# Active-expert loop with the next block's transposes, split and first products issued in the current block, and first weights loaded in routing

## The chip, the cores and the metric

The kernel runs on one core of one Trainium2 chip. The metric is device time in microseconds (us) of one execution; the figure for a kernel is the median of its runs.

## The reference, cut to what matters

Sixteen sequences of 512 tokens of width 256 (8192 tokens) pass an adaptive layer norm and attention, then a second one and a mixture of experts. Only the latter is touched by the change:

```python
logits = x @ Wr + br                                  # 8 experts
top_vals, top_idx = jax.lax.top_k(logits, TOPK)       # TOPK = 2
w = jax.nn.softmax(top_vals, axis=-1)
cap = max(int(math.ceil(N / E * CF)), 1)              # 1280
kv, ki = jax.lax.top_k(key_mat, cap)                  # per expert, its cap largest weights
tok = flat_tok[ki]
gate = jnp.where(valid, w_flat[ki], 0.0)
h1 = jax.nn.gelu(einsum('ech,ehf->ecf', x[tok], W1) + b1, approximate=False)
y = einsum('ecf,efh->ech', h1, W2) + b2
out = jnp.zeros_like(x).at[tok.reshape(-1)].add((y * gate[..., None]).reshape(-1, H))
```

W1 is 256 x 1024 and W2 1024 x 256 for each expert, in float32. The router's weights are small (0.001) beside its bias, so with the inputs drawn here the two experts with the largest bias, numbers 2 and 4, take the tokens. Each is full at its capacity of 1280. The others get none.

## The kernel before

The program is written engine by engine; semaphores set the order between engines, and each engine runs its own instructions in the order written. Stages follow one another behind a barrier: `setup`, `attention`, `route`, `experts`, `last_norm`.

`route` finds each expert's tokens. On VectorE (DVE) it computes keys, then the 1280th largest key of each expert in 15 steps of counting, then the number of blocks per expert (L1059 to L1063), then the table INFO (L1066 to L1076): for each of the eight experts the number of its blocks, the blocks before it, and the active experts before it. A loop of one-hot products on TensorE, with operands from DVE and GpSimd (POOL), then gives the list IDX of token numbers (L1093 to L1106).

`experts` works in blocks of 256 tokens (BLK), five for a full expert. `each` (L1154) is the loop that every engine runs: over all eight experts, three reads from INFO each, and for those with blocks an optional `expert` part, then an inner loop of `block` parts. A counter g numbers the blocks across experts. A `Stream` (L37) is a semaphore that is waited for with a value computed from g.

Each matrix is kept as the sum of a high part (float32r) and a low part. `hi_lo_matmul` (L89) makes three matmuls of one product. An expert's part: SyncE (SP) loads W1F and W2F (1 MB each), ScalarE (ACT) writes the high parts W1H and W2H, DVE the low parts W1L and W2L. A block's part:

- POOL (L1210) copies the token numbers to TOKG, gathers the tokens' rows to XG (two indirect DMAs) and their keys to GK (two more). Then it waits for YS of the block before and adds it to `acc_rows` in HBM with two accumulating scatters by the token numbers TOKS. Each scatter is waited for before the next one is issued. `gate(j)` (L1194) is a tiny POOL operation that carries waits.
- TensorE (L1302) transposes XG to PSUM (four), then `mm1(f)` for eight columns of W1 and, two steps behind, `mm2(f)` with W2. Both are groups of six matmuls.
- DVE (L1267) splits the transposed tokens into XTH and XTL, takes the gates from GK, makes YB = b2 x gate, splits each gelu output HF into HH and HL, and finally writes YS = y x gate + YB (L1295).
- ACT (L1249) applies gelu, with a load of the activation tables before a block's first one.

On TensorE the order within a block is this:

```python
for f in range(FC + 2):
    if f < FC:
        mm1(f)
    if f >= 2:
        mm2(f - 2)
```

Its first `mm1` waits for XTL, so for transposes and split, and its transposes stand behind the last `mm2` of the block before.

Of the kernel before, what the change touches and what calls it, by code (L numbers as in the profile page):

```python
# [17 lines left out]
F32, F32R = mybir.dt.float32, mybir.dt.float32r  # L18
# [92 lines left out]
def build_program(nc, ap, out):  # L111
    top = ExitStack()
    with top:
# [33 lines left out]
        m["INFO"] = sb("INFO", [1, 4 * E], I32)  # L147
# [683 lines left out]

def route(nc, ap, m, sem, sb):
# [34 lines left out]
    NBR, NBD = sb("NBR", [1, 6, E]), sb("NBD", [P, E])  # L867
    ktab = m["ktab_dram"]
# [3 lines left out]
    s_db, s_ab, s_oe = sem("s_rdb"), sem("s_rab"), sem("s_roe")  # L872
# [9 lines left out]
    with nc.Block() as block:  # L882
# [41 lines left out]
        @block.sync  # L924
        def _(sp):
            sp.wait_ge(s_key, TC)
# [42 lines left out]
        def _(dve):  # L969
# [97 lines left out]
            nb, act_, cum, cua, z = (NBR[:, j, :] for j in range(5))  # L1067
            link(dve.tensor_copy(nb, nb_ps[0:1, :]))
            link(dve.tensor_scalar(act_, nb, 0.0, None, ALU.is_gt))
            link(dve.memset(z, 0.0))  # L1070
            link(dve.tensor_tensor_scan(cum, nb, z, 0.0, ALU.add, ALU.add))
            link(dve.tensor_tensor_scan(cua, act_, z, 0.0, ALU.add, ALU.add))
            link(dve.tensor_tensor(cum, cum, nb, ALU.subtract))
            link(dve.tensor_tensor(cua, cua, act_, ALU.subtract))
            for j, row in enumerate((nb, cum, cua)):
                link(dve.tensor_copy(m["INFO"][:, j * E:(j + 1) * E], row))  # L1076
# [34 lines left out]
def experts(nc, ap, m, sem, sb):  # L1111
# [4 lines left out]
    GATES_USED = 4 + BT  # L1116
    assert CAP % BLK == 0

    W1F, W2F = sb("W1F", [P, KC, F]), sb("W2F", [P, FC, D])
# [3 lines left out]
    B1R, B1, B2 = sb("B1R", [E * FC, P]), sb("B1", [P, E * FC]), sb("B2", [P, E, D])  # L1123

    XG, GK, TOKG, TOKS = sb("XG", [P, BT, D]), sb("GK", [P, BT, E]), sb("TOKG", [P, BT], U32), sb("TOKS", [P, BT], U32)
# [10 lines left out]
    s_w1, s_w2 = S("fw1", 1, 16), S("fw2", 1, 16)  # L1136
# [3 lines left out]
    s_tokg, s_toks = S("ftokg", BT), S("ftoks", 1)  # L1140

    s_t, s_m1, s_m2, s_gate, s_yb = S("ft", 1), S("fm1", FC), S("fm2", FC), S("fgate", BT), S("fyb", BT)
    s_xh, s_xl, s_gelu, s_hh, s_hl, s_y = S("fxh", KC), S("fxl", KC), S("fgelu", FC), S("fhh", FC), S("fhl", FC), S("fy", BT)
    s_init, s_b, s_b1t, s_b1 = sem("finit"), sem("fb"), sem("fb1t"), sem("fb1")
# [9 lines left out]
    def each(eng, expert, block):  # L1154


        with eng.Fori(0, E) as e:
            nb = eng.value_load(INFO[0:1, bass.ds(e, 1)], min_val=0, max_val=MAXB)
            g0 = eng.value_load(INFO[0:1, bass.ds(e + E, 1)], min_val=0, max_val=E * MAXB)
            a = eng.value_load(INFO[0:1, bass.ds(e + 2 * E, 1)], min_val=0, max_val=E)  # L1160
            with eng.If(nb > 0):
                if expert is not None:
                    expert(e, a, g0)
                if block is not None:
                    with eng.Fori(0, nb) as k:
                        block(e, a, g0 + k, k)

    with nc.Block() as blk:
        @blk.sync
        def _(sp):  # L1170
            w1 = ap["L0_ffn_W1"].rearrange("e (k p) f -> p (e k) f", p=P)
            w2 = ap["L0_ffn_W2"].rearrange("e (f p) n -> p (e f) n", p=P)
            sp.dma_start(B1R[:, :], ap["L0_ffn_b1"].rearrange("e (f p) -> (e f) p", p=P)).then_inc(s_b, 16)
            sp.dma_start(B2[:, :, :], ap["L0_ffn_b2"].partition_broadcast(P)).then_inc(s_b, 16)

            def expert(e, a, g):
                k_row, f_row = sp.snap(e * KC), sp.snap(e * FC)

                s_w1l.wait(sp, a, -1)
                s_w1.done(sp.dma_start(W1F[:, :, :], w1[:, bass.ds(k_row, KC), :]))  # L1180
                s_w2l.wait(sp, a, -1)
                s_w2.done(sp.dma_start(W2F[:, :, :], w2[:, bass.ds(f_row, FC), :]))
            each(sp, expert, None)

        @blk.gpsimd
        def _(pool):
            start(pool, streams)

            pool.iota(TOKS[:, :].bitcast(I32), pattern=[[0, BT]], base=NT, channel_multiplier=1).then_inc(s_init, 1)
            pool.memset(YS[:, :, :], 0.0).then_inc(s_init, 1)  # L1190
            pool.memset(GATE[:, :], 0.0).then_inc(s_init, 1)
            pool.wait_ge(s_init, 3)
# [5 lines left out]
            def scatter(g):  # L1198


                s_y.wait(pool, g, -1)
                for t in range(BT):
                    if t:
                        s_sc.wait(pool, g, t - 1)
                    gate(4 + t)
                    off = bass.IndirectOffsetOnAxis(ap=TOKS[:, t:t + 1], axis=0)
                    s_sc.done(pool.indirect_dma_start(out=m["acc_dram"], out_offset=off, in_=YS[:, t, :], in_offset=None,
                                                      compute_op=ALU.add))

            def block(e, a, g, k):  # L1210

                s_toks.wait(pool, g, -1)
                gate(0)
                for t in range(BT):
                    s_tokg.done(pool.tensor_copy(TOKG[:, t:t + 1], IDX[:, bass.ds(e * (CAP // P) + k * BT + t, 1)]))
                s_tokg.wait(pool, g, BT - 1)
# [10 lines left out]

                scatter(g)
# [237 lines left out]
```

## Time and profile before

| | us |
|---|---|
| median of 3 runs | 1643.86 |
| lowest and highest | 1641.98, 1646.58 |
| profiled execution: its own time | 1649.5 |
| its span | 1647.7 |
| TensorE matmuls busy | 1333.9 (81%) |
| DVE busy | 1141.7 (69%) |
| ACT busy | 742.3 (45%) |
| POOL busy | 531.9 (32%) |

Times in the profile count from the start of the span. The page cuts the span into 40 slices and gives each engine's busy tenths. The timeline lists instructions in order of time with the idle time before each and what ended it; "issue" is idle time in which the engine waited for nothing that the profile shows. A POOL row DMA_INDIRECT is the time in which POOL writes the descriptors, not the transfer. TensorE's granted clock (PEclk) is 1.00 or 0.50 of full speed, or a mean of the two over a window.

### The profile page before, as it was taken

The page shows a single profiled execution, that of the slowest core. Times are in us where ns is not written, and L with a number is a line of the kernel's source. Part 1 is how long each engine was busy: PE and PEld are TensorE (multiplying, and loading weights), DVE is VectorE, ACT ScalarE, POOL GpSimd, SP SyncE. Part 2 cuts the span into 40 slices and gives each one's busy share as a digit, 9 for nine tenths or more (in the row PEclk, how much of TensorE's full clock was granted, in tenths as well). Part 3 has the DMA queues.
Part 4 walks back from the last instruction along what each step waited for, and adds up shares of the span by engine and source line. Part 5 has one row for each costly group of instructions (what it writes and reads, how often), then busy time and mean ns, then how long its engine had stood idle before and what let it go on. Part 6 is the DMA issues. An engine that isn't in the chain of part 4 may idle for free. (4 is left out here: it accounts for less than half of the span.)

```text
span 1647.7 us, 24318 instructions
## 1 busy us (share of the span) xinstructions
PE 1333.9 (81%) x5919; PEld 946.5 (57%) x5920; DVE 1141.7 (69%) x2504; ACT 742.3 (45%) x1433; POOL 531.9 (32%) x853
## 2 busy tenths in 40 slices
PE   5499999999999999999999999998311948868200
PEld 3366666666666666666666666665211947867200
DVE  2478778777787778787787877875377525555387
ACT  2365656556566565565655657544000013232052
POOL 1111413324234232342323413313300544455147
PEclk8699999999999999999999999999555558988655
DMA  4000011010010110101101011011000032111364
GB/s 107 14 13 27 3 51 52 0 51 26 26 51 0 52 41 11 52 0 51 52 0 51 0 39 40 1 39 39 26 6 1 0 104 62 27 32 29 111 215 143
DMA packets 66758, 67.90 MB, mean 41 GB/s; under 512 B 13504, under 2 KB 62832, under 8 KB 66560
## 3 DMA queue, kind: packets, MB, share of 16 engines
q1 hardware_dynamic: 42960, 42.72, 8.6%
q10 hardware_dynamic: 18960, 18.88, 3.4%
q0 software_dynamic: 4768, 5.59, 2.2%
q14 instruction: 53, 0.43, 0.1%
q8 instruction: 17, 0.28, 0.1%
HBM read 38.25 MB, written 28.66 MB: 41 GB/s over the span
## 5 line engine op out<-in xcount | busy, mean ns | idle before, releaser
L827 PE MATMUL PS<-PF,V 128*128 128x512 f32 x1024 | 524.0, 594 | 0.0
L558 ACT ACTIVATE PF<-PS 128x512 f32<-128x512 f32 x512 | 302.9, 595 | 345.4 <-PE PS L753 343.7
L730 DVE TENSOR_REDUCE NMAX<-PS 128x1 f32<-128x512 f32 x512 | 346.4, 686 | 160.1 <-PE PS L762 149.7
L752 PE MATMUL PS<-Q,K 128*128 128x512 f32 x512 | 405.8, 793 | 0.9 <-ACT PF L558 0.9
L528 POOL TENSOR_TENSOR XL<-XF,XH 128x512 fp32r<-128x512 f32 x64 | 84.2, 1315 | 445.6 <-ACT XH L633 445.6
L762 PE MATMUL PS<-K,Q 128*128 128x512 f32 x512 | 203.3, 398 | 6.9 <-DVE NMAX L730 6.2
L753 PE MATMUL PS<-Q,K 128*128 128x512 f32 x512 | 202.7, 396 | 0.0
L827 PEld LDWEIGHTS PS<-PF,V 128*128 128x128 f32 x1024 | 174.5, 189 | 36.2 <-issue 6.6
L576 ACT ACTIVATE Q<-PS 64x512 fp32r<-64x512 f32 x256 | 151.5, 592 | 64.8 <-PE PS L93 60.0
L752 PEld LDWEIGHTS PS<-Q,K 128*128 128x128 f32 x512 | 97.2, 190 | 123.5 <-issue 105.6
L753 PEld LDWEIGHTS PS<-Q,K 128*128 128x128 f32 x512 | 97.4, 190 | 121.7 <-issue 121.6
L762 PEld LDWEIGHTS PS<-K,Q 128*128 128x128 f32 x512 | 96.6, 189 | 31.6 <-DVE NMAX L730 8.6
L669 DVE STREAM_TRANSPOSE RECT<-PS 64x512 f32<-64x512 f32 x128 | 91.9, 718 | 13.0 <-PE PS L827 9.2
L520 POOL TENSOR_TENSOR NLO<-TR,NHI 128x512 fp32r<-128x512 f32 x32 | 41.1, 1286 | 163.9 <-DVE NHI L714 163.9
L698 DVE TENSOR_TENSOR Q<-PS,Q 64x512 fp32r<-64x512 f32 x128 | 87.7, 685 | 7.7 <-ACT Q L576 4.7
L681 DVE TENSOR_TENSOR XF<-PS,RECT 64x512 f32<-64x512 f32 x128 | 87.2, 681 | 7.6 <-DVE RECT L675 4.6
L675 DVE STREAM_TRANSPOSE RECT<-RDEN 64x512 f32<-64x512 f32 x128 | 89.1, 696 | 1.0
L536 POOL TENSOR_TENSOR H<-H,MODB 128x256 f32<-128x256 f32 x64 | 47.0, 734 | 109.1 <-ACT H L625 109.1
L91 PE MATMUL PS<-GH,XH 128*128 128x256 f32 x256 | 74.0, 289 | 6.4 <-POOL XL L528 4.6
L93 PE MATMUL PS<-GH,XL 128*128 128x256 f32 x256 | 73.5, 287 | 0.0
L92 PE MATMUL PS<-GL,XH 128*128 128x256 f32 x256 | 73.5, 287 | 0.0
L91 PE MATMUL PS<-XTH,W1H 128*128 128x256 f32 x160 | 51.6, 323 | 24.6 <-DVE XTL L1274 23.3
(272 smaller groups left out, 2463.1 us busy)
## 6 DMA issues: line engine op xcount, KB each, us to landing
X<-in_L_attn_x SPq DMA_DIRECT2D x16, 512.0 KB, 5.0
MODB<-mod_rows SPq DMA_DIRECT2D x16, 512.0 KB, 4.5
h_rows<-H ACTq DMA_DIRECT2D x16, 512.0 KB, 3.4
acc_rows<-H ACTq DMA_DIRECT2D x16, 512.0 KB, 4.1
A<-acc_rows SPq DMA_DIRECT2D x16, 512.0 KB, 9.1
out_x<-X SPq DMA_DIRECT2D x16, 512.0 KB, 2.9
Q<-MROW SPq DMA_DIRECT2D x128, 2.0 KB
W1F<-in_L_ffn_W SPq DMA_DIRECT2D x2, 1024.0 KB
```

The lines of the kernel that those rows point to most:

```text
L91: eng.matmul(out, lhs[0], rhs[0], start=first, stop=False)
L558: s_exp.done(act.activation(PF[:, u % 4, :], st_bank(u), ACT.Exp))
L576: s_qhi.done(act.activation(Q1[half * R:(half + 1) * R, 2 * idx + odd, :], bank[odd * R:(odd + 1) * R, :], ACT.Copy))
L669: s_x.done(dve.transpose(RECT[:, :], bank[R:P, :]))
L675: s_x.done(dve.transpose(RECT[:, :], RDEN[:, :].unsqueeze(2).broadcast_to([R, T // 32, 32])))
L681: s_x.done(dve.tensor_tensor(XF[odd * R:(odd + 1) * R, p % 2, :], bank[0:R, :], RECT[:, :], ALU.mult))
L698: s_qlo.done(dve.tensor_tensor(Q2[0:R, h, :], bank[odd * R:(odd + 1) * R, :], Q1[odd * R:(odd + 1) * R, h, :].bitcast(F32), ALU.subtract))
L730: s_mred.done(dve.tensor_reduce(NMAX[:, h % 2, c:c + 1], mx_bank(u), AX.X, ALU.max, negate=True))
L752: pe.matmul(st_bank(u), K1[:, kp, keys], Q1[:, h, :], start=True, stop=False)
L753: s_st.done(pe.matmul(st_bank(u), K2[:, kp, keys], Q2[:, h, :], start=False, stop=True))
L762: s_mx.done(pe.matmul(mx_bank(u), Q1[:, h, c * P:(c + 1) * P], K1[:, kp, :], start=True, stop=True))
L827: s_pv.done(pe.matmul(pv_bank(h), V1[:, vp, c, :], PF[:, u % 4, :], start=(c == 0), stop=(c == TC - 1)))
```

## The change

- The table INFO now lists the active experts only, in order: number, blocks less one, and blocks before; then the count of active experts and of blocks. An active expert has at least two blocks. DVE computes it with more small operations.
- In `route`, SP loads the biases (B1R, B2) at the start and the first active expert's W1F and W2F once INFO is written. Later SP loads the next expert's weights when the low parts of the current ones are made (after the last one, it loads once more, a transfer that no product uses).
- `each` loops over active experts: a `first` part, `middle` for all blocks but the last, and `last`, a second copy of the block's code.
- TensorE does the next block's transposes in the middle of the current block (behind `mm1(4)`), and its `mm1(0)` and `mm1(1)` behind the current block's last `mm2`. DVE splits the next block's tokens before YS. The gates are taken behind f = 2.
- POOL keeps the token numbers of two blocks more (TOKG to TOKP to TOKQ to TOKS). Its turn g gathers for block g and scatters block g-2, the first scatter ahead of the GK gathers. Two turns without gathers follow the last block. DVE writes YS of block g when turn g+1 has scattered block g-1.
- ACT runs a one-column activation (DUMMY) at the start of each part, so that the load of the tables stands there.

The core of the diff:

```diff
+            sp.wait_ge(s_info, 1)
+            e = sp.value_load(m["INFO"][0:1, 0:1], min_val=0, max_val=E - 1)
+            w1, w2 = weight_rows(ap)
+            k_row, f_row = sp.snap(e * KC), sp.snap(e * (F // P))
+            m["s_w1"].done(sp.dma_start(m["W1F"][:, :, :], w1[:, bass.ds(k_row, KC), :]))
+            m["s_w2"].done(sp.dma_start(m["W2F"][:, :, :], w2[:, bass.ds(f_row, F // P), :]))
...
+    def each(eng, first, middle, last):
+        with eng.Fori(0, actives(eng)) as a:
+            e = eng.value_load(INFO[0:1, bass.ds(a, 1)], min_val=0, max_val=E - 1)
+            more = eng.value_load(INFO[0:1, bass.ds(a + E, 1)], min_val=1, max_val=MAXB - 1)
+            g0 = eng.value_load(INFO[0:1, bass.ds(a + 2 * E, 1)], min_val=0, max_val=E * MAXB)
+            if first is not None:
+                first(e, a, g0)
+            with eng.Fori(0, more) as k:
+                middle(e, a, g0 + k, k)
+            last(e, a, g0 + more, more)
...
+            def shift(g):
+                s_toks.wait(pool, g, -1)
+                gate(4 + BT)
+                s_tokg.done(pool.tensor_copy(TOKQ[:, :], TOKP[:, :]))
+                s_tokg.wait(pool, g, 0)
+                gate(5 + BT)
+                s_tokg.done(pool.tensor_copy(TOKP[:, :], TOKG[:, :]))
+                s_tokg.wait(pool, g, 1)
+                gate(6 + BT)
+            def take(g):
+                s_toks.done(pool.tensor_copy(TOKS[:, :], TOKQ[:, :]))
+                s_toks.wait(pool, g, 0)
+                s_y.wait(pool, g, -BT - 1)
...
+                shift(g)
...
+                take(g)
+                scatter(g, 0)
...
+                for t in range(1, BT):
+                    s_sc.wait(pool, g, t - 1)
+                    scatter(g, t)
+                s_gx.wait(pool, g, 0)
+                s_gk.wait(pool, g, 0)
+                gate(0)
...
+                if more:
+                    split_tokens(g + 1)
...
+                s_sc.wait(dve, g + 1, BT - 1)
...
+            def expert(e, a, g):
+                transposes(g)
                 s_w1l.wait(pe, a, 0)
...
+                mm1(g, 0)
+                mm1(g, 1)
...
+            def block(e, a, g, more):
+                for f in range(2, FC):
+                    mm1(g, f)
+                    if f == 4 and more:
+                        transposes(g + 1)
+                    mm2(a, g, f - 2)
+                mm2(a, g, FC - 2)
+                mm2(a, g, FC - 1)
+                if more:
+                    mm1(g + 1, 0)
+                    mm1(g + 1, 1)
```

POOL in the block's loop, before. GATEp is the tile of `gate`, the names in brackets are the semaphores waited for (fsc: a scatter has landed, fy: YS is written, fgate: the gates are read):

```order
L1196 TENSOR_TENSOR GATEp<-GATEp 128x1 [waits ftoks]
...
L1215 COPY TOKG<-IDX 128x1
...
L1196 TENSOR_TENSOR GATEp<-GATEp 128x1 [waits ft,ftokg]
L1221 DMA XG<-h_rows,TOKG 128x256 x2
...
L1196 TENSOR_TENSOR GATEp<-GATEp 128x1 [waits fgate]
L1226 DMA GK<-key_rows,TOKG 128x8 x2
L1196 TENSOR_TENSOR GATEp<-GATEp 128x1 [waits fy]
L1207 DMA acc_rows<-YS,TOKS 8320x256
...
L1196 TENSOR_TENSOR GATEp<-GATEp 128x1 [waits fsc]
L1207 DMA acc_rows<-YS,TOKS 8320x256
...
L1196 TENSOR_TENSOR GATEp<-GATEp 128x1 [waits fsc]
L1231 COPY TOKS<-TOKG 128x2
```

and now:

```order
L1245 COPY TOKQ<-TOKP 128x2
...
L1231 TENSOR_TENSOR GATEp<-GATEp 128x1 [waits ftokg]
L1248 COPY TOKP<-TOKG 128x2
...
L1231 TENSOR_TENSOR GATEp<-GATEp 128x1 [waits ftokg]
...
L1268 DMA XG<-h_rows,TOKG 128x256 x2
L1254 COPY TOKS<-TOKQ 128x2
...
L1231 TENSOR_TENSOR GATEp<-GATEp 128x1 [waits fy]
L1238 DMA acc_rows<-YS,TOKS 8320x256
...
L1231 TENSOR_TENSOR GATEp<-GATEp 128x1 [waits fgate]
L1275 DMA GK<-key_rows,TOKG 128x8 x2
...
L1231 TENSOR_TENSOR GATEp<-GATEp 128x1 [waits fsc]
L1238 DMA acc_rows<-YS,TOKS 8320x256
```

The first scatter has moved ahead of the GK gathers, and the wait for it (fsc) behind them. Two copies and their gates are new before the XG gathers, and one copy behind them.

TensorE around a block's edge, before. The last second group, and the next turn of the loop:

```order
L91 MATMUL PS<-W2H,HH 128x256 [waits fhl]
L92 MATMUL PS<-W2L,HH 128x256
L93 MATMUL PS<-W2H,HL 128x256
...
L1165 REGISTER_ALU
L1165 COMPARE_AND_BRANCH
...
L1307 MATMUL PS<-IDENT,XG 128x128 [waits fxl]
L1307 MATMUL PS<-IDENT,XG 128x128 x3
...
L91 MATMUL PS<-XTH,W1H 128x256 [waits fxl]
L92 MATMUL PS<-XTL,W1H 128x256
```

and now:

```order
L91 MATMUL PS<-W2H,HH 128x256 [waits fhl]
L92 MATMUL PS<-W2L,HH 128x256
L93 MATMUL PS<-W2H,HL 128x256
...
L91 MATMUL PS<-XTH,W1H 128x256 [waits fxl]
L92 MATMUL PS<-XTL,W1H 128x256
L93 MATMUL PS<-XTH,W1L 128x256
...
L91 MATMUL PS<-XTH,W1H 128x256 [waits fgelu]
L92 MATMUL PS<-XTL,W1H 128x256
L93 MATMUL PS<-XTH,W1L 128x256
...
L1200 REGISTER_ALU
L1200 COMPARE_AND_BRANCH
```

The next block's first groups (they wait for fxl, the low part of its tokens) follow the last second group directly, with no transposes between, and the loop turns behind them. The transposes stand between `mm1(4)` and `mm2(2)`.

## Rows read from the trace of the kernel before

**Rows 1.** The page's 40 slices of 41.2 us: busy tenths of TensorE.

```profile
PE   5499999999999999999999999998311948868200
```

**Rows 2.** Timeline, DVE, POOL: start, duration (us), instruction, [idle before, releaser].

```profile
1335.92 0.24 DVE L1106 SCALAR_TENSOR_TENSOR IDX<-PS,LF 128x80 uint32<-128x80 f32 x1
...
1540.37 0.18 POOL L1196 TENSOR_TENSOR GATEp<-GATEp 128x1 f32<-128x1 f32 x1 [2.39 <-DMA acc_rows<-YS,TOKS]
```

**Rows 3.** Waits, 1337 to 1545 us: total us, times, longest.

```profile
POOL GATEp L1196 <- DMA acc_rows<-YS,TOKS: 49.3, 21, 2.9
...
PE PS L91 <- DVE XTL L1274: 23.3, 9, 4.7
```

**Rows 4.** Timeline, TensorE: the inner turn, and one group in mid-block.

```profile
1375.44 0.60 PE L1307 MATMUL PS<-IDENT,XG 128*128 128x128 f32 x4
...
1434.29 0.28 PE L91 MATMUL PS<-XTH,W1H 128*128 128x256 f32 x1
...
1435.00 0.28 PE L91 MATMUL PS<-W2H,HH 128*128 128x256 f32 x1
```

**Rows 5.** Timeline, DVE: YS of blocks 0 and 4 (starts of ten such rows).

```profile
1375.70 0.88 DVE L1295 SCALAR_TENSOR_TENSOR YS<-PS,GATES,YB 128x256 f32<-128x256 f32 x2 [1.14 <-PE PS L93]
...
1441.95 0.88 DVE L1295 SCALAR_TENSOR_TENSOR YS<-PS,GATES,YB 128x256 f32<-128x256 f32 x2 [1.13 <-PE PS L93]
```

**Rows 6.** Windows: us, busy by engine, PEclk, DMA share, GB/s.

```profile
1411.00:1427.00 16.00, 13.94 (x100) 13.29 (x100) 7.58 (x24) 4.96 (x9) 8.04 (x15) 0.89 0.21 33
1468.00:1486.00 18.00, 12.90 (x103) 12.01 (x101) 9.87 (x30) 4.86 (x9) 9.21 (x16) 1.00 0.19 30
```

**Rows 7.** Timeline, POOL: one turn, blocks 1 and 2.

```profile
1385.15 0.18 POOL L1196 TENSOR_TENSOR GATEp<-GATEp 128x1 f32<-128x1 f32 x1 [2.35 <-DMA acc_rows<-YS,TOKS]
...
1386.84 1.02 POOL L1221 DMA_INDIRECT XG<-h_rows,TOKG  x1 [0.33 <-issue]
...
1389.16 0.21 POOL L1196 TENSOR_TENSOR GATEp<-GATEp 128x1 f32<-128x1 f32 x1
...
1392.88 0.19 POOL L1196 TENSOR_TENSOR GATEp<-GATEp 128x1 f32<-128x1 f32 x1 [1.08 <-DVE YS L1295]
...
1397.24 0.18 POOL L1196 TENSOR_TENSOR GATEp<-GATEp 128x1 f32<-128x1 f32 x1 [2.40 <-DMA acc_rows<-YS,TOKS]
...
1401.43 0.18 POOL L1196 TENSOR_TENSOR GATEp<-GATEp 128x1 f32<-128x1 f32 x1 [2.23 <-DMA acc_rows<-YS,TOKS]
```

**Rows 8.** Timeline, DVE in routing: 64 elements; INFO table begins, ends.

```profile
1190.75 0.22 DVE L991 TENSOR_TENSOR DENr<-M 128x64 f32<-128x64 f32 x1
...
1269.06 0.15 DVE L1068 COPY NBR<-PS 1x8 f32<-1x8 f32 x1 [1.50 <-PE PS L954]
...
1270.92 0.69 DVE L1080 TENSOR_REDUCE D<-PS 128x64 f32<-128x512 f32 x1
```

**Rows 9.** Timeline, POOL and TensorE: first gate, first product.

```profile
1345.94 0.19 POOL L1196 TENSOR_TENSOR GATEp<-GATEp 128x1 f32<-128x1 f32 x1 [7.14 <-issue]
...
1360.66 0.58 PE L91 MATMUL PS<-XTH,W1H 128*128 128x256 f32 x1 [4.22 <-DVE XTL L1274]
```

**Rows 10.** Timeline, POOL and TensorE: a gather waited for.

```profile
1513.35 1.26 POOL L1221 DMA_INDIRECT XG<-h_rows,TOKG  x1 [0.47 <-issue]
...
1517.91 0.65 PE L1307 MATMUL PS<-IDENT,XG 128*128 128x128 f32 x4 [0.27 <-DMA XG<-h_rows,TOKG]
```

**Rows 11.** Timeline, TensorE: second expert's first products, half clock.

```profile
1453.00 0.58 PE L91 MATMUL PS<-XTH,W1H 128*128 128x256 f32 x1 [4.72 <-DVE XTL L1274]
...
1453.60 0.41 PE L93 MATMUL PS<-XTH,W1L 128*128 128x256 f32 x1
1453.81 0.41 PE L91 MATMUL PS<-XTH,W1H 128*128 128x256 f32 x1
```

**Rows 12.** Groups by line, 1337:1545: busy us, mean ns, idle before.

```profile
L1307 PE MATMUL PS<-IDENT,XG 128*128 128x128 f32 x40 | 7.1, 307 | 18.1 <-DMA XG<-h_rows,TOKG 12.8 <-issue 5.3
...
L1263 DVE TENSOR_TENSOR W1L<-W1F,W1H 128x2048 fp32r<-128x2048 f32 x2 | 4.6, 2292 | 22.0 <-issue 17.3 <-ACT W1H L1245 4.6
```

More of the change, by code:

```diff
@@ L1152, in y_bank, with actives @@
         return PS[:, 5 + t, 0:D]
[L1154 to L1166, printed above, removed]
+    def actives(eng):
+        return eng.value_load(INFO[0:1, 3 * E:3 * E + 1], min_val=1, max_val=E)
+    def each(eng, first, middle, last):
[8 more added lines that the diff above has]
+            last(e, a, g0 + more, more)
     with nc.Block() as blk:
@@ L1194, in gate, with scatter @@
             def gate(j):
                 pool.tensor_tensor(GATE[:, j:j + 1], GATE[:, GATES_USED:], GATE[:, GATES_USED:], ALU.add)
[L1198 to L1208, printed above, removed]
+            def scatter(g, t):
+                gate(4 + t)
+                off = bass.IndirectOffsetOnAxis(ap=TOKS[:, t:t + 1], axis=0)
+                s_sc.done(pool.indirect_dma_start(out=m["acc_dram"], out_offset=off, in_=YS[:, t, :], in_offset=None,
+                                                  compute_op=ALU.add))
@@ L1308, in block @@
                 s_t.done(last)
-                s_w1l.wait(pe, a, 0)
-                def mm1(f):
-                    s_gelu.wait(pe, g, max(f - 4, -1))
-                    cols = slice(f * P, (f + 1) * P)
-                    for c in range(KC):
-                        if f == 0:
-                            s_xl.wait(pe, g, c)
-                        last = hi_lo_matmul(pe, h_bank(f), (W1H[:, c, cols], W1L[:, c, cols]),
-                                            (XTH[:, c, :], XTL[:, c, :]), c == 0, c == KC - 1)
-                    s_m1.done(last)
@@ L1321, in mm2 @@
-                def mm2(f):
-                    if f == 0:
-                        s_w2l.wait(pe, a, 0)
-                        s_y.wait(pe, g, -1)
-                    s_hl.wait(pe, g, f)
-                    for t in range(BT):
-                        rows = slice(t * P, (t + 1) * P)
-                        last = hi_lo_matmul(pe, y_bank(t), (HH[:, f % 4, rows], HL[:, f % 4, rows]),
-                                            (W2H[:, f, :], W2L[:, f, :]), f == 0, f == FC - 1)
-                    s_m2.done(last)
@@ L1331, in block, with mm1 @@
-                for f in range(FC + 2):
-                    if f < FC:
-                        mm1(f)
-                    if f >= 2:
-                        mm2(f - 2)
+            def mm1(g, f):
+                s_gelu.wait(pe, g, f - 4)
+                cols = slice(f * P, (f + 1) * P)
+                for c in range(KC):
+                    if f == 0:
+                        s_xl.wait(pe, g, c)
+                    last = hi_lo_matmul(pe, h_bank(f), (W1H[:, c, cols], W1L[:, c, cols]),
+                                        (XTH[:, c, :], XTL[:, c, :]), c == 0, c == KC - 1)
+                s_m1.done(last)
@@ new lines, in mm2, with expert @@
+            def mm2(a, g, f):
+                if f == 0:
+                    s_w2l.wait(pe, a, 0)
+                    s_y.wait(pe, g, -1)
+                s_hl.wait(pe, g, f)
+                for t in range(BT):
+                    rows = slice(t * P, (t + 1) * P)
+                    last = hi_lo_matmul(pe, y_bank(t), (HH[:, f % 4, rows], HL[:, f % 4, rows]),
+                                        (W2H[:, f, :], W2L[:, f, :]), f == 0, f == FC - 1)
+                s_m2.done(last)
+            def expert(e, a, g):
+                transposes(g)
+                s_w1l.wait(pe, a, 0)
+                mm1(g, 0)
+                mm1(g, 1)
@@ L1338, in _ @@
             pe.wait_ge(s_b1, 1)
[L1339 removed]
+            each(pe, expert, lambda e, a, g, k: block(e, a, g, True), lambda e, a, g, k: block(e, a, g, False))
 def last_norm(nc, out, m, sem, sb):
```

152 lines of the change are left out of this document (92 added, 60 removed).

## The prediction, made before the changed kernel was run

> **What bounds the kernel now.** The page's 40 slices come first [rows 1]: TensorE is full until slice 29, idle in routing, then busy for 6 to 8 tenths over the experts. The change lies there and in a few routing rows. The experts stage runs from IDX at 1336.2 us to the landing of the last scatter (gate before it at 1540.37, plus 4.2 as below: 1544.6) [rows 2]: 208 us for ten blocks of 256 tokens, five for each of two experts. The waits of that stretch [rows 3] name two pairs: TensorE waits 23.3 us for XTL, and POOL waits 49.3 us, 21 times, for its scatters. So the next views are both timelines.
>
> TensorE: a group of six matmuls takes 0.71 us at full clock (1434.29 to 1435.00) [rows 4]. A block has 16 groups and four transposes (0.6): 12.0 us. But YS to YS is (1441.95 - 1375.70)/4 = 16.6 us [rows 5]. The 4.6 us between are the hole at the block's edge: transposes, split, first product, and gelu with its table load before the first second product. A stretch at half clock in most blocks adds to it (0.89 granted in one window, 1.00 in another) [rows 6].
>
> POOL: one turn goes from the gate at 1385.15 to that at 1401.43 [rows 7]. It is 1.7 us to the first gather, 2.3 for two XG gathers, 2.6 for two GK gathers, then 4.36 and 4.2 for the scatters, each waited for until it lands (2.4 and 2.2 us idle), with 1.08 idle for YS ahead of them. So POOL alone needs 15.2 us. It hides just behind 16.6; a faster TensorE meets it at once.
>
> **The change, part by part.**
> Routing. The INFO table takes DVE from 1269.06 to 1270.92: ten small operations, 0.18 us apart [rows 8]. Now there are eleven such (2.0), two and then three of 64 elements (0.22 for that size, 0.25 with the gap: 1.25), a reduction of 192 (between 0.22 for 64 and 0.69 for 512: 0.4) and a cast (0.2): 3.85. DVE has no idle before the next operation, so all of it is path: **+2.0**; with every new operation at 0.18 it is +1.3, with all six larger ones at 0.4 about +3. The weight and bias transfers issued there meet no other large one, and SP's wait for INFO holds only SP: nothing.
>
> Head. POOL's table walk passes the inactive experts 0 and 1, nine loads in the 7.14 us ahead of its first gate [rows 9]: 0.8 us each. Now there are four: -4.0. With +2.0 and 0.1 for the second IOTA, the first turn starts at 1344.0. W1F has landed in routing, and W1H and W1L are done before XG, which is last: first gather at 1346.4, landed 4.3 later (1513.35 to 1517.91 shows 4.56 with issues slower by 0.3 [rows 10]), transposes 1.1, split 0.8. The first product comes near 1353 where it was 1360.66 [rows 9].
>
> POOL's new turn. The GK gathers (2.6) now stand between the two scatters and fill the 2.4 us wait: -2.4. Two copies (0.26 with their wait) and net two gates (0.2) are added: +1.0, of it 0.65 before the first gather. The new waits for gx and gk fall inside the second scatter's wait: nothing; without that cover they would cost no more than one gate. So 15.2 - 2.4 + 1.0 = **13.8 us**. Bounds: 12.6 where the overlap is whole and the additions are free, 16.2 where nothing overlaps. I take 13.8: the same instructions go to the same queue, only their order differs, and their issue times are the most regular rows of the trace.
>
> TensorE's new cycle. The next block's split and first products are ahead of the block's edge. XTL comes some 0.5 late, behind HL of f = 7, so TensorE needs 12.5 us of its own. Gelu's table load (1.28) runs while the last three second groups do (2.1): hidden. But the transposes in block g need XG of g+1, and these are gathered in the POOL turn that starts when YS of g-1 may be written: 2.35 + 4.3 after that, then 0.6 and nine groups of 0.71: 13.65. YS comes 0.3 behind, which POOL does not need for another 4.7 us. So POOL's turn sets the period, 13.8 where 16.6 was, and TensorE waits about 2.5 us for XG. A half-clock stretch after it costs up to 1.7 us and is taken from the next wait.
>
> **The sum**, in the profile's time. Turn 0 is 0.6 longer, for one scatter wait of 2.9 instead of 2.3 while weights land [rows 3]: 1344.0 + 14.4 = 1358.4. Five more turns: 1427.4. YS of block 4 has waited for that and ends at 1428.4. The second expert starts cold: three loads 2.3, W1L 2.3 [rows 12], half the split 0.8, first product at 1433.8. (Before, YS at 1441.95 to the product at 1453.00 was 11.0 [rows 5, 11]; now it is 6.3, from 1427.5.) Three groups at half clock, six matmuls of 0.213 each [rows 11], take 3.8; gelu 0.65, HH and HL 0.71 and gates 0.3 follow: 1439.3. Turn 6 holds GK until these gates are read; then 2.6, 0.3 and 4.2, so it ends at 1446.5 where 1441.2 was possible. Three turns: 1487.9. The two late turns have no gathers: 0.8 for a load, 1.85, 0.35 and 8.6 give 11.6, the second 10.7. The last YS is ready for it: 1488.9 + 0.75 + 13 x 0.71 + 1.3 = 1500.2. Landing at 1510.2 instead of 1544.6: **-34.4 us**, some two thirds of it from the period. The last stage only moves.
>
> The profiled execution took 1649.5 us (its span is 1647.7), 5.6 over the median of 1643.86. On the median that makes 1643.86 - 34.4 = **1609.5 us**. Within 0.3% (5 us) a measurement of this kernel cannot tell a change from none.
>
> **The rivals.**
> (a) No overlap: the gathers behind an accumulating scatter delay it, or the wait moves to the second scatter. The turn goes up to 16.2: 9 x 2.4 = +22, 1631; with half of it 1620. For it: a wait of 2.9 beside other traffic [rows 3]. Against: the experts' transfers use 0.19 to 0.21 of the DMA engines' time [rows 6].
> (b) POOL's turn is shorter and TensorE's 12.5 or 12.7 rules: 9 x 1.1 = -10, 1599.5. For it: no row shows an added copy above 0.26. Against: the walk of waits around them has its own register work.
> (c) TensorE loses time at each loop turn. At the outer turn it sat idle 5.3 us with nothing but issue to blame [rows 12]; at the inner turn there is no gap: the transposes at 1375.44 carry no idle time [rows 4]. If the longer code brought 5.3 to each of 8 inner turns, the cycle would be 17.8: 8 x 4.0 = +32, 1641.5, no change. Against: the inner body keeps its 100 matmuls. The Trainium skill (Runtime: NRT & Kernel Launch, Instruction fetch mechanics) says that a taken branch to a page outside the fetched window stalls for a fetch. By that rule the outer body, doubled, could pay once at its turn back, and the sum would rise by one such idle time, to 1615; no row here separates a fetch from the table loads at that place.
> (d) **Slower**: the clock. Two shorter waits in a block, for YS and for XG, replace one long one, and TensorE may stay at its lower level (1.2 GHz). A block of 16 groups of 1.28 plus 1.1 is 21.6 us: 9 x 7.8 = +70, 1680. It decides once a period passes 13.8 + 34.4/9 = 17.6, with over half of each block at half clock (12.5 + 9.1 x 0.56). Against: with a hole in every block, the clock granted was still 0.89 and 1.00 [rows 6].
>
> **How the numbers follow.** The forecast, with turns of 13.3 to 14.6 (1605 to 1617), has 0.62; (a) 0.17; (b) 0.15; (c) 0.03; (d) 0.03. The range 1598 to 1625 holds the forecast, (b) and about half of (a). Faster: the forecast, (a) and (b), 0.93, rounded down for what I have not thought of; same 0.04; slower 0.03.
>
> **What would show it.** Right: the gate before the second scatter no longer idles for acc_rows, only the one behind it; almost no idle for YS on POOL; YS 13.8 us apart; TensorE waits for XG, not for XTL; the first product near 1353; YS of block 4 to the next product near 6 us; turn 6 stretched by the gates. Wrong: YS under 13 us apart (b), idle for acc_rows twice in a turn (a), issue idle at each inner turn (c), a granted clock under 0.7 over the blocks (d).

## The result, and the profile after

The changed kernel takes **1625.22 us** (median of 4 runs, 1621.00 to 1628.07) against 1645.15 us for the kernel before in the same set (4 runs, 1641.98 to 1646.58): a ratio of 0.9879, 95% interval 0.9852 to 0.9907. It is faster, and the gain is 19.9 us where 34.4 were forecast. In a later set of runs it took 1625.31 us against 1650.50 us (0.9852, 0.9835 to 0.9869): 25.2 us. The two medians of the kernel after lie within a microsecond; those of the kernel before lay between 1642.5 and 1651.0 (1642.5 and 1645.8 on chip 0, 1650.5 to 1651.0 on chips 5 and 6).

The stage itself can be read more exactly than the whole. From the write of IDX to the first load of the accumulated rows the profile before has 1551.03 - 1335.92 = 215.1 us, the one after 189.9 us, so the change is worth **25.2 us** in its stage. The table INFO ahead of that stretch costs 2.1 us more than before (the rows stand with the two kernels run again, below), which leaves 23.1 us. The forecast for the same stretch was 178.7 us (landing at 1510.2, 6.4 us to that load, IDX at 1337.9). These are the ends of it after, from the timelines of VectorE, GpSimd and SyncE (columns as in [rows 2]):

```profile
1338.27 0.24 DVE L1136 SCALAR_TENSOR_TENSOR IDX<-PS,LF 128x80 uint32<-128x80 f32 x1
...
1521.50 0.18 POOL L1231 TENSOR_TENSOR GATEp<-GATEp 128x1 f32<-128x1 f32 x1 [2.25 <-DMA acc_rows<-YS,TOKS]
1528.14 26.64 SPq L1463 DMA_DIRECT2D A<-acc_rows  x16
```

The page's line of TensorE's 40 slices, beside [rows 1]: the stage of the experts is fuller where it was 6 to 8 tenths, and one slice in its middle, the change of expert, is still low.

```profile
PE   6499999999999999999999999999511595979200
```

The waits from 1340 to 1530 us, beside [rows 3]:

```profile
POOL GATEp L1231 <- DMA acc_rows<-YS,TOKS: 29.6, 16, 2.4
...
PE PS L1382 <- DMA XG<-h_rows,TOKG: 22.6, 7, 14.4
...
PE PS L91 <- DVE XTL L1337: 11.0, 10, 8.5
DVE YS L1370 <- DMA acc_rows<-YS,TOKS: 7.9, 3, 6.4
```

GpSimd waits 29.6 us for its scatters where it waited 49.3, TensorE 11.0 us for XTL where it waited 23.3, and there is no line for GpSimd waiting for YS (8.4 us at most once, 31.1 in all before). TensorE now waits for XG: of its 22.6 us, 14.4 are the start, and 8.2 fall in six later places, where the kernel before had 0.3 in one. Of the 11.0 us for XTL, 8.5 are one wait at the change of expert. One turn of GpSimd, from its timeline, beside [rows 7]:

```profile
1375.04 0.53 POOL L1231 TENSOR_TENSOR GATEp<-GATEp 128x1 f32<-128x1 f32 x2 [2.31 <-DMA acc_rows<-YS,TOKS]
...
1377.37 1.01 POOL L1268 DMA_INDIRECT XG<-h_rows,TOKG  x1 [0.42 <-issue]
...
1379.78 0.20 POOL L1254 COPY TOKS<-TOKQ 128x2 uint32<-128x2 uint32 x1
1380.14 0.20 POOL L1231 TENSOR_TENSOR GATEp<-GATEp 128x1 f32<-128x1 f32 x1 [0.17 <-POOL TOKS L1254]
1380.86 1.62 POOL L1238 DMA_INDIRECT acc_rows<-YS,TOKS  x1 [0.52 <-issue]
...
1382.96 1.00 POOL L1275 DMA_INDIRECT GK<-key_rows,TOKG  x1 [0.16 <-issue]
...
1385.24 0.21 POOL L1231 TENSOR_TENSOR GATEp<-GATEp 128x1 f32<-128x1 f32 x1
1385.61 1.62 POOL L1238 DMA_INDIRECT acc_rows<-YS,TOKS  x1 [0.16 <-issue]
...
1389.35 0.53 POOL L1231 TENSOR_TENSOR GATEp<-GATEp 128x1 f32<-128x1 f32 x2 [1.84 <-DMA acc_rows<-YS,TOKS]
```

The gate at 1385.24, ahead of the second scatter, has no idle time for acc_rows any more: the GK gathers cover the first scatter's flight in full. But the turn is 14.31 us, not 13.8. The reader should see two idle times that the sum did not have: 0.17 before the gate at 1380.14 and 0.52 before the first scatter; in the kernel before, the gate of [rows 7] at 1392.88 was followed by its scatter after 0.15.

YS comes 13.5, 14.3, 14.3 and 17.4 us apart in the first expert. The last of these waits for the scatter of a GpSimd turn that has walked the outer loop on its way; VectorE's row and GpSimd's row at that place:

```profile
1420.57 0.44 POOL L1231 TENSOR_TENSOR GATEp<-GATEp 128x1 f32<-128x1 f32 x1 [2.28 <-issue]
...
1435.45 0.88 DVE L1370 SCALAR_TENSOR_TENSOR YS<-PS,GATES,YB 128x256 f32<-128x256 f32 x2 [6.39 <-DMA acc_rows<-YS,TOKS]
```

Laid beside the forecast, the starts of GpSimd's turns (the gate behind a landing) give the whole miss of the stage:

| part | forecast | measured | difference |
|---|---|---|---|
| first gate | 1344.0 | 1344.1 | +0.1 |
| turn 0 | 14.4 | 15.8 | +1.4 |
| turns 1 to 4 | 55.2 | 58.2 | +3.0 |
| turn 5 (outer turn in it) | 13.8 | 17.4 | +3.6 |
| turn 6 | 19.1 | 19.6 | +0.5 |
| turns 7 to 9 | 41.4 | 43.6 | +2.2 |
| two late turns | 22.3 | 22.8 | +0.5 |
| last landing | 1510.2 | 1521.5 | +11.3 |

### The profile page after: what moved, and what is told of

Read it like the earlier page. It is cut to its first block and busy times, and to the rows that moved or that the text cites. A ratio compares the mean times of both kernels' runs of the same rounds, so it can differ in the third digit from the quotient of the medians.

```text
span 1623.7 us, 24084 instructions
## 1 busy us (share of the span) xinstructions
PE 1327.1 (82%) x5919; PEld 937.7 (58%) x5920; DVE 1145.3 (71%) x2512; ACT 740.7 (46%) x1442; POOL 556.0 (34%) x928
## 5 line engine op out<-in xcount | busy, mean ns | idle before, releaser
L1318 ACT ACTIVATE HF<-PS,B 128x256 f32<-128x256 f32 x80 | 37.9, 474 | 104.0 <-PE PS L93 94.2
L922 POOL TENSOR_TENSOR OA<-OE,TOK 128x640 f32<-128x640 f32 x16 | 33.1, 2071 | 115.3 <-DVE OE L1127 115.3
```

## The experiments

The two theories that the first eight runs tell apart. **P**: GpSimd's turn still sets the period, and the missing 11 us are in its turns. **T**: TensorE (with VectorE behind it) is already the bound, and the forecast overrated what it can do. Beside each time stands, as "stage", the time from IDX to the first load of the accumulated rows in that run's profile (189.9 for the kernel after), since it does not depend on where the program's start happened to end. Two profiles of one kernel differ in it by 0.4 to 1.1 us (188.8 in the second profile of the kernel after). The runs were taken in sets on different chips, so two medians of different sets are compared with more caution than two stages.

### The GK gathers ahead of the scatters again

```diff
+                s_gate.wait(pool, g, -1)
+                gate(2)
+                for t in range(BT):
...
                 take(g)
                 scatter(g, 0)
-                s_gate.wait(pool, g, -1)
-                gate(2)
-                for t in range(BT):
...
```

> Edit: GpSimd issues the two GK gathers ahead of the first scatter again, in the kernel after; nothing else moves. Theory P (GpSimd's turn sets the period of the blocks, 14.3 us from landing to landing): about 2.4 us of issue no longer lie beside the first scatter's flight, the turn grows to 16.3 to 16.7, the gate before the second scatter idles for acc_rows again (some 1.9 to 2.1 us), and the time grows by 17 to 22 us over the kernel after, to about 1644, so nearly the whole gain of the change is gone. Theory T (TensorE or VectorE sets 14.3, and GpSimd has slack): the waits move, the time stays within 3 us of the kernel after.

Measured: 1655.50 us (5 runs), ratio 1.0079 (1.0060 to 1.0097), stage 216.7 us. This is slower than the kernel before, also in the stage (215.1 and 215.5 us there): the whole gain of the change hangs on this order. By the medians it is 13 us slower, by the stage and the table only 3 to 4; the rest lies outside both and is open, as for the medians further down. The rows of GpSimd's timeline in that kernel show the idle time of a scatter's flight back before each second scatter (2.20 before the gate at 1381.93), as in [rows 7]:

```profile
1378.11 1.62 POOL L1238 DMA_INDIRECT acc_rows<-YS,TOKS  x1 [0.51 <-issue]
1381.93 0.18 POOL L1231 TENSOR_TENSOR GATEp<-GATEp 128x1 f32<-128x1 f32 x1 [2.20 <-DMA acc_rows<-YS,TOKS]
```

Six of the nine intervals of YS are 16.5 to 17.2 us, some 2.4 more than after. The 26.8 us of the stage (30.3 by the medians) are more than the 17 to 22 expected. Turn 0 grew by 5.5 us, with waits of 2.4 and 4.6 for its two scatters, and turn 6 by 3.8, because the first GK gather now stands ahead of the next scatter and waits 6.0 us for the gates of the block before; the other turns with gathers grew by 1.2 to 2.8 each. Theory P holds, T is out.

### The second scatter's wait behind the next XG gathers

```diff
+                s_sc.wait(pool, g, -1)
+                gate(3)
                 take(g)
                 scatter(g, 0)
...
                 gate(0)
-                s_sc.wait(pool, g, BT - 1)
-                gate(3)
```

> Edit: in the kernel after, GpSimd waits for the second scatter's landing only behind the next turn's two XG gathers (just before TOKS is overwritten) and not at the turn's end; one added gather at the start raises the scatters' semaphore by 16, so that every wait of it is on a positive number. Theory P (GpSimd's turn of 14.3 us sets the period): XG's two issues (2.1 us) come to lie beside the second scatter's flight, GpSimd's own turn falls to about 12.2, and what rules next is TensorE or VectorE at 12.5 to 13.7: 6 to 18 us less than after over the ten turns, 1607 to 1619 us, forecast 1612. Theory T (the other engines are at their limit at 14.3 already): within 3 us of the kernel after, and GpSimd then waits for YS.

Measured: 1613.62 us (5 runs), ratio 0.9821 (0.9803 to 0.9840), stage 177.4 us: 12.5 us less than the kernel after. YS comes every 13.05 us in six of its nine intervals. The window from 1376 to 1402 us of that kernel (columns as in [rows 6]) has TensorE busy for 25.14 of 26 us at full clock, and GpSimd waits for YS and for gates there; over the whole stage its waits for scatters are 9.7 us where they were 29.6:

```profile
1376.00:1402.00 26.00, 25.14 (x201) 23.88 (x201) 17.66 (x53) 10.56 (x20) 20.11 (x42) 1.00 0.25 41
```

So 13.05 us is TensorE's own cycle, 0.5 more than the 12.5 of the prediction, and in the kernel after TensorE has 1.3 us of slack in each turn of 14.3.

### TensorE's transposes late again, in both kernels

```diff
                     mm1(g, f)
-                    if f == 4 and more:
-                        transposes(g + 1)
...
                 if more:
+                    transposes(g + 1)
                     mm1(g + 1, 0)
```

> Edit: in the kernel after, TensorE transposes the next block behind the last second product of the current one, not behind the fifth first product; VectorE's split follows it. GpSimd's order is unchanged. Theory P (GpSimd's turn of 14.3 us sets the period, TensorE has 1.2 to 1.5 us of slack in a block): TensorE's path grows by transposes, split and two semaphore steps, 1.5 to 2.3 us a block, of which the slack takes most: 0 to 0.8 us a block, 0 to 7 us in all. Theory T (the early transposes and products are what shortened the block): the whole 1.5 to 2.3 us a block shows, 13 to 21 us, 1638 to 1646.

> Edit: the scatter's wait moved as in the run with ratio 0.982, and TensorE's transposes behind the last second product as in the run of this call that changes only that. Theory: with GpSimd's turn at 12.2 us and TensorE's block at 13.05, TensorE is the bound, so the 1.5 to 2.3 us of transposes, split and waits show in full at each of the eight blocks that have a next one: 12 to 18 us over the late-wait kernel, 1626 to 1632, while the same edit on the kernel after costs a third of that or less. Rival: the edit costs the same in both kernels, so the bound wasn't what changed between them.

Measured: on the kernel after 1627.48 us (4 runs; 0.9863, 0.9839 to 0.9887), stage 190.7: +0.8 us (+1.9 against the second profile of the kernel after). On the late-wait kernel 1621.63 us (5 runs; 0.9819, 0.9795 to 0.9842), stage 183.5: +6.1 us, with YS 14.3 us apart in five of nine intervals, 1.3 more than without the edit. The same edit costs next to nothing where GpSimd rules and 1.3 us in most blocks where TensorE does. That is less than the 1.5 to 2.3 a block and the 12 to 18 us in all that were expected. This is the clean test of which engine is the bound, and it also tells that the part of the change that looks largest in the diff, the transposes and split issued inside the block, carries almost nothing of its gain as it stands. TensorE's timeline in the late-wait kernel shows the wait that the late split brings, once a block:

```profile
1388.41 0.39 PE L91 MATMUL PS<-XTH,W1H 128*128 128x256 f32 x1 [1.08 <-DVE XTL L1342]
```

### Where the 0.5 us of each turn go

```diff
                 shift(g)
+                s_toks.done(pool.tensor_copy(TOKS[:, :], TOKQ[:, :]))
...
-                take(g)
+                s_toks.wait(pool, g, 0)
+                s_y.wait(pool, g, -BT - 1)
                 scatter(g, 0)
```

> Edit: in the kernel after, GpSimd copies TOKQ to TOKS ahead of the XG gathers instead of behind them; the gate and the first scatter follow the second XG gather directly. Theory S (the 0.5 us between the gate and the first scatter, which my sum took at 0.15, is the scatter's own preparation on GpSimd's sequencer, and it shows only because two short instructions stand ahead of it and cover nothing): that idle falls to 0.15 to 0.2, the 0.17 us in which the gate waits for the copy goes too, and the turn falls from 14.3 to 13.7 to 13.9, near the 13.8 of my sum; over eight full turns the time falls by 3 to 5 us, to about 1621. Rival R (the 0.5 us belongs to the register work of the wait for YS, whatever stands ahead): idle and turn stay, time within 1.5 us of after.

Measured: 1619.39 us (5 runs), ratio 0.9814 (0.9793 to 0.9836), stage 182.2: 7.7 us less than after. Seven full turns are 13.8 to 14.2 us long (start of TOKQ's copy to the next), where the same seven are 14.3 to 15.0 in the kernel after. GpSimd's timeline shows the gate and the scatter directly behind the gather:

```profile
1379.60 0.95 POOL L1269 DMA_INDIRECT XG<-h_rows,TOKG  x1 [0.31 <-issue]
1380.57 0.21 POOL L1231 TENSOR_TENSOR GATEp<-GATEp 128x1 f32<-128x1 f32 x1
1380.94 1.69 POOL L1238 DMA_INDIRECT acc_rows<-YS,TOKS  x1 [0.16 <-issue]
```

Rival R is out: the register work of the wait for YS is still there, in the same place, and the idle time is gone. What changed is that a gather of 0.95 us stands ahead of the gate instead of a copy of 0.2 us. Theory S fits. That the 0.5 us are the scatter's own preparation is its reading of this; no run takes that time apart. The gain is more than the 3 to 5 us expected: the seven full turns give 4.8, the other turns of the stage 2.9, of which 0.6 in the first late turn, which varies as much between the two profiles of the kernel after (11.5 and 10.9 us).

### The weights' loads in the stage of the experts again

```diff
             w1, w2 = weight_rows(ap)
+            e = sp.value_load(m["INFO"][0:1, 0:1], min_val=0, max_val=E - 1)
+            k_row, f_row = sp.snap(e * KC), sp.snap(e * (F // P))
+            m["s_w1"].done(sp.dma_start(m["W1F"][:, :, :], w1[:, bass.ds(k_row, KC), :]))
+            m["s_w2"].done(sp.dma_start(m["W2F"][:, :, :], w2[:, bass.ds(f_row, F // P), :]))
             nact = actives(sp)
```

The same lines, and the two loads of the biases, leave the routing.

> Edit: in the kernel after, the biases and the first expert's weights are loaded at the start of the experts as in the kernel before, not in the routing. Theory: routing ends 1.5 to 2 us earlier (no table loads on SyncE ahead of its last steps), and the first product waits for weights that land about 1350 to 1353 and then for W1L; the first XG gather's packets queue among those of the weights. If the part of the change that moves the loads is worth what I summed (head -4.0, of which loads about -2, against +2.2 in routing), the time stays within 2 us of after. Rival: the loads set the first product (in the kernel before it was at 1360.7, after at 1355.9): 3 to 6 us slower than after.

Measured: 1631.06 us (6 runs), ratio 0.9927 (0.9910 to 0.9944), stage 192.6: 2.7 us slower by the stage (3.8 against the second profile of the kernel after), 5.8 by the medians of two sets. This is nearer the rival's 3 to 6 than the theory's 2, though not by the way that the rival named: the first product came 16.4 us behind IDX, *earlier* than the 17.8 after. What came later was the end of GpSimd's turn 0 (20.2 us long instead of 16.2), and in a kernel whose period is GpSimd's turn, that is what counts.

### Two things that slow GpSimd's first turn

In the kernel after, the first XG gather takes 2.85 us to issue instead of 1.01, while W1L is computed; GpSimd's and VectorE's timelines:

```profile
1346.31 2.85 POOL L1268 DMA_INDIRECT XG<-h_rows,TOKG  x1 [0.58 <-issue]
...
1345.74 2.29 DVE L1341 TENSOR_TENSOR W1L<-W1F,W1H 128x2048 fp32r<-128x2048 f32 x1 [7.23 <-ACT W1H L1307]
```

```diff
-                s_w1l.done(dve.tensor_tensor(W1L[:, :, :], W1F[:, :, :], W1H[:, :, :].bitcast(F32), ALU.subtract))
+                for j in range(8):
+                    c = slice(j * P, (j + 1) * P)
+                    last = dve.tensor_tensor(W1L[:, :, c], W1F[:, :, c], W1H[:, :, c].bitcast(F32), ALU.subtract)
+                s_w1l.done(last)
```

> Edit: in the kernel after, VectorE computes W1L and W2L in 8 instructions of an eighth each instead of one of 2.29 us. Theory D (GpSimd's writing of gathers and scatters stands still while one long VectorE instruction on the weights runs; it took 2.85 us instead of 1.02 for the first XG gather, 3.36 instead of 1.62 for a scatter at the change of expert): these two fall to 1.1 to 1.5 and 1.7 to 2.1, and the time falls by 2 to 4 us, to 1621 to 1623. Rival Q (what slows them is in the DMA queue, the weights' transfer or the table loads): both stay as long, and the time stays or grows by the 14 added instructions' fixed costs, 0 to 1.5 us.

Measured: 1624.28 us (4 runs), ratio 0.9885 (0.9864 to 0.9906), stage 188.0. The mechanism of theory D is there:

```profile
1349.39 2.77 DVE L1343 TENSOR_TENSOR W1L<-W1F,W1H 128x256 fp32r<-128x256 f32 x8 [7.24 <-ACT W1H L1307]
...
1349.95 1.32 POOL L1268 DMA_INDIRECT XG<-h_rows,TOKG  x1 [0.58 <-issue]
1351.58 1.42 POOL L1268 DMA_INDIRECT XG<-h_rows,TOKG  x1 [0.30 <-issue]
...
1357.64 1.11 PE L1387 MATMUL PS<-IDENT,XG 128*128 128x128 f32 x4 [14.61 <-DMA XG<-h_rows,TOKG]
```

The gathers take 1.3 and 1.4 us beside the pieces, and the scatter at the change of expert 1.62 instead of 3.36. But the time fell by 0.9 us and the stage by 1.9 (0.8 against the second profile of the kernel after), where 2 to 4 were expected. The gathers now landed late: the transposes come 6.1 us behind the second gather's issue, 4.4 in the kernel after. The Trainium skill (SBUF — State Buffer, SBUF: two separate sides) states that a VectorE operation that holds the port pair it shares with GpSimd keeps GpSimd from writing its transfers' descriptors until it ends. The rows agree with that: W1L ends at 1348.03, and the gather's issue ends 1.13 us later, about its own 1.01 after the end of W1L.

The last run asks what held the packets. As soon as W1L is done, SyncE loads the next expert's W1F (1 MB), in the kernel after at 1348.21, while the first gather is still being issued. In the kernel with pieces it goes at 1352.34, during the second gather's issue, and in the 6 us from there the DMA engines are busy for 0.76 of the time (the last but one figure, columns as in [rows 6]):

```profile
1352.00:1358.00 6.00, 0.36 (x2) 0.37 (x3) 0.16 (x1) 0.66 (x2) 4.79 (x7) 0.50 0.76 238
```

```diff
                 s_w1l.wait(sp, a, 0)
+                g0 = sp.value_load(INFO[0:1, bass.ds(a + 2 * E, 1)], min_val=0, max_val=E * MAXB)
+                s_gx.wait(sp, g0, 0)
                 s_w1.done(sp.dma_start(W1F[:, :, :], w1[:, bass.ds(k_row, KC), :]))
```

> Edit: on the kernel with W1L and W2L in eight pieces, SyncE issues the next expert's W1F load only when the first XG gathers of the current expert have landed, not as soon as W1L is computed. In that kernel GpSimd's gathers were no longer held up (1.3 and 1.4 us to issue), and yet the first transposes came 6.1 us after the second gather's issue; in the late-wait kernel with pieces, where the gathers' packets went out before the load, they came 3.1 us after. Theory X (the 1 MB load's packets hold XG's up, 3 us at the first block): the first transposes come 3 to 3.5 us after the second issue again, the first product some 14.7 to 15.2 us behind the write of IDX instead of 17.8, and the stage from IDX to the first load of the accumulated rows falls from 188.0 by 1 to 3 us (GpSimd's turn 0 is not all behind XG). Rival Y (gathers at the program's first block are slow for another reason): 17.8 and 188 again.

Measured: 1628.95 us (4 runs), ratio 0.9901 (0.9885 to 0.9918), stage 192.1. Theory X is right on the gathers: transposes 3.0 us behind the second issue, first product 14.9 us behind IDX, 3.0 earlier. And the stage is 4.1 us *longer* (4.7 by the medians). The packets of the W1F load now lie beside the first scatter, and those of the W2F load, which follows W2L, beside the second, so each of them lands 6.6 and 6.1 us after its issue instead of some 4, and GpSimd waits for both:

```profile
1353.38 0.38 SPq L1217 DMA_DIRECT2D W1F<-in_L_ffn_W  x1
...
1359.12 0.37 SPq L1219 DMA_DIRECT2D W2F<-in_L_ffn_W  x1
...
1359.12 0.19 POOL L1233 TENSOR_TENSOR GATEp<-GATEp 128x1 f32<-128x1 f32 x1 [2.29 <-DMA acc_rows<-YS,TOKS]
1359.47 1.62 POOL L1240 DMA_INDIRECT acc_rows<-YS,TOKS  x1
...
1365.61 0.54 POOL L1233 TENSOR_TENSOR GATEp<-GATEp 128x1 f32<-128x1 f32 x2 [4.30 <-DMA acc_rows<-YS,TOKS]
```

Turn 0 went from 15.7 to 19.4 us. The first product is not the bound of the head; the end of turn 0 is.

### The best version, and the two kernels again

> Edit: both the scatter's wait behind the next XG gathers (ratio 0.982 alone) and W1L and W2L in eight pieces each (1 to 2 us alone). If the long VectorE instruction holds GpSimd's gathers up at the change of expert, and TensorE sets the rest of the stage at 13.05 us a block, the two gains stand at different places (turn 0 and turn 6 against the eight others) and add: 1611 to 1613. Rival: where TensorE sets the pace, the first XG gather of an expert has slack and the pieces only add their fixed costs: 1613.5 to 1615.

> The fastest kernel so far (the scatter's wait behind the next XG gathers, W1L and W2L in eight pieces), now beside after on the same chip: from IDX to the first load of the accumulated rows 175 us against after's 190, so 12 to 16 us faster than after, ratio to before 0.976 to 0.982.

Measured for the late wait with the pieces: 1612.89 us (5 runs; 0.9773, 0.9750 to 0.9795), and again, beside the kernel after, 1613.17 us (5 runs; 0.9774, 0.9757 to 0.9790), 12.1 us less than the 1625.31 of after in the same set. The stage is 175.3 and 175.8 us, 1.6 to 2.1 less than with the late wait alone (177.4); by the times the two cannot be told apart. In this kernel the second XG gather is issued before W1L is done and the W1F load goes, and the transposes come 3.1 us behind it.

> The kernel after, unchanged, a second profile and time beside the runs of before. In the ten profiles so far the write of IDX came at 1335.9 (before) and 1338.3 to 1342.5 us (changed kernels), and all of that difference stands before the routing: from the write of the routing's table to that of IDX it is 65.3 to 65.6 us in every one. Theory N (the start of the program varies from execution to execution, by some us, whatever the kernel): the second profile of before has IDX anywhere in 1336 to 1343, and after is 20 to 26 us faster than before, as the stage of the experts is (25 us from IDX to the first load of the accumulated rows). Rival C (the changed kernel pays 2 to 4 us at its start, by its longer program or its other layout of memory): before again at 1336 or less, after again at 1339 to 1342, and the gain is 20.

> The kernel before, unchanged. Theory N: IDX anywhere in 1336 to 1343, from IDX to the first load of the accumulated rows 215 us again within 1. Rival C: IDX at 1334 to 1337.

Measured: after 1625.31 us (5 runs), before 1650.72 us (12 runs, ratio to the other runs of the same kernel 0.9999, 0.9987 to 1.0010). IDX at 1338.2 in after and 1339.2 in before; stage 188.8 and 215.5 us. The kernel before has moved by 3.3 us where it stood at 1335.9, and the changed kernel stands where it stood. So the start of the program does move from execution to execution, as theory N has it: the first product of attention with V comes at 82.4 to 86.7 us, at 82.4 and at 85.5 in the two profiles of the kernel before.

That is not all of it, though. From that product to IDX the kernel before takes 1253.5 and 1253.7 us and the changed kernels 1255.7 to 1255.8 in eleven of twelve profiles. (The twelfth is the first profile of after with 1251.9; its way to the table was 3.8 us shorter, and its granted clock from 1150 to 1170 us was 0.82 where before has 0.50.) The 2.1 us between them are the table INFO. A measure from "the write of the routing's table" begins behind the table's own operations and can't see them. VectorE's rows in the kernel after, beside [rows 8]: the table's first operation, its last, and the next step of the routing:

```profile
1269.34 0.16 DVE L1085 COPY NBR<-IOT 1x8 f32<-1x8 f32 x1 [1.49 <-PE PS L971]
...
1272.96 0.17 DVE L1105 CAST INFO<-TABLE 1x26 int32<-1x26 f32 x1
...
1273.27 0.69 DVE L1110 TENSOR_REDUCE D<-PS 128x64 f32<-128x512 f32 x1
```

The table takes 3.93 us there (3.91 to 3.93 in all changed kernels) against 1.86 and 1.85 in the kernel before, and from its end to IDX all fourteen profiles have 65.0 us. So rival C is right in part: the changed kernel does pay 2.1 us before IDX, by its table and not by its start.

## Why the prediction was right, and where it was wrong

The direction, the place and the mechanism were right: a GpSimd turn that no longer waits for its first scatter sets a shorter period, and TensorE waits for XG. Of the list of what would show it, the gate without idle time, the missing wait for YS and TensorE's wait for XG came as written; YS came 14.3 and not 13.8 us apart. YS of block 4 to the next product was 5.8 us, near the 6 forecast, and the gates did stretch turn 6 (19.6 us, forecast 19.1). The size was wrong: 25.2 us of the stage's 36.4 (34.4 and the 2.0 of routing), and 1625.2 us is just above the top of the range, 1625. What failed is the pricing of GpSimd's path, in its turn, at the outer loop and at the head:

- **"15.2 - 2.4 + 1.0 = 13.8"** was mis-sized in the 1.0: it priced two copies and two gates by their own durations and took the idle time ahead of the scatter (0.15 behind a long instruction or a wait) as fixed. Behind two short instructions it is 0.52, and the gate waits 0.17 for the copy. The run with the copy moved gave 13.8 to 14.2. Over turns 1 to 4 and 7 to 9 the miss is 5.2 us of the 11.3; the two idle times make 3.8 of it, and the rest is mostly in turns 1 and 7 (15.1 and 14.8 us), for which no run isolates a cause.
- **"Five more turns: 1427.4"** left a step out. The outer loop's three table loads on GpSimd (2.28 us idle for issue at 1420.57) were counted for TensorE at the change of expert, not for GpSimd, which by the prediction's own argument was the bound: +2.3 of turn 5's 3.6.
- **The head, "landed 4.3 later"**: the first gate came at 1344.1 as forecast, the first product at 1356.0 instead of 1353. The prediction set W1H and W1L "done before XG, which is last", and did not ask what they would do to XG: W1L held the issue for 1.8 us, and the W1F load that it released, 8 us earlier than before, held the packets. Turn 0 took 1.4 more.
- **Routing, "+2.0"**, was right: VectorE's table takes 3.93 us where it took 1.86, so +2.07, and its parts came as priced (the eleven small operations 2.0, the five of 64 elements 1.2, the reduction with its gap 0.4, the cast 0.3). IDX came 2.35 later in the profile after; the other 0.28 are the difference of the two executions up to the table.
- **"TensorE needs 12.5 us of its own"**: 13.05, by the late-wait kernel. It cost nothing here, since GpSimd's turn is longer.
- **Rival (a)**, no overlap, is excluded: the first scatter's flight is covered in full. **Rival (b)** is excluded: YS came 14.3 us apart, and 13.05 only once the wait for the second scatter had moved. **Rival (c)**: no idle time at the inner turns on TensorE. The Trainium skill (Runtime: NRT & Kernel Launch, Instruction fetch mechanics) would let a longer outer body stall once; TensorE's transposes at the change of expert waited 2.0 us for issue in the kernel after, less than the 5.3 of before, so no run here shows an added one. **Rival (d)**: the granted clock was 1.00 from 1376 to 1405, 0.92 from 1436 to 1500 and 0.91 over all of 1356 to 1521, not under 0.7.
- On the median: of the 15.7 us between 1609.5 and 1625.2, 11.3 are the stage and the table (23.1 us gained where 34.4 were forecast). The other 4.4 are the base. The forecast was taken from a median of three runs of the kernel before, 1643.9; beside the later runs of the kernel after the same kernel took 1650.5, while the kernel after took 1625.3 both times. The medians of the kernel before lie up to 8.5 us apart from set to set, lower on chip 0 than on chips 5 and 6, and within a set its slower executions show the lower mean granted clock (in one set on chip 0, 1639.6 us at 0.886 and 1646.2 at 0.877). Why is open.

## What to carry to other kernels

When a change moves the bound to a queue with hand-made order, price that queue's turn once more from zero: every loop level it walks, every short instruction that leaves idle time ahead of the next transfer, and every long operation of a neighbour that can hold it. Then test which engine is the bound by making another engine worse: an edit that costs nothing in one version and 1.3 us a block in another says more than a busy share. And a transfer that is delayed to clear one path lands on the next one; ask which of the two sets the end. When you compare two kernels between marks, set the first mark ahead of everything that the change touches; here a mark behind the table hid 2.1 us that the forecast had right.

## What was not expected of the hardware

- The same indirect scatter on GpSimd had 0.52 us of idle time ahead of it where a copy and a gate of 0.2 us stood before it, and 0.16 where a gather of 0.95 us and the gate did.
- A 2.29 us VectorE subtraction with both inputs and its output in SBUF stretched a gather's issue from 1.01 to 2.85 us and a scatter's from 1.62 to 3.36; in eight pieces it stretched them hardly or not at all (1.3 and 1.62).
- A 1 MB load on SyncE's queue delays GpSimd's row gathers by 3 us (6.1 instead of 3.0 to 3.1 from the second issue to the transposes) and scatters by some 2 us each (6.1 to 6.6 instead of some 4 us to land). The DMA engines were busy for 0.76 of the 6 us behind the load in the kernel with pieces, against 0.23 in the window 1376 to 1405 of the kernel after, in which no weights are loaded: a mean over the stage hides this.
